# A tree stage on one core: matmul operands padded with zeros to 128 rows, and a sorted tile's last two sums moved from VectorE to GpSimd

## What is computed

```
h = h + _L1_ffn_ref(_layernorm(h), w1s, b1s, w2s, b2s)
# in _L1_ffn_ref, for each token, from the root down, 8 levels:
score  = flat_x . w1s[current] + b1s[current]
choice = (sign(score) + 1) / 2
current = current * 2 + choice + 1
# then, over the 8 nodes of its path:
out += (flat_x @ w2s[node] + b2s[node]) * gelu(|score|)
```

## Time and profile before

| | us |
|---|---|
| median of 3 runs | 4308.63 (4298.92 to 4319.09) |
| the profiled execution | 4311.47 |
| its span, first to last instruction | 4309.1 |
| TensorE busy | 3519.4 (82%) |
| VectorE busy | 2653.5 (62%) |
| ScalarE busy | 2259.2 (52%) |
| GpSimd busy | 696.7 (16%) |
| mean granted clock, share of 2.4 GHz | 0.822 |

### The profile page before, as it was taken

One profiled execution on the slowest core, in us unless ns is written; L12 is line 12 of the kernel. 1 busy time (PEld: TensorE's weight loads), 2 busy tenths in 40 slices (PEclk: granted clock), 3 DMA queues, 4 the chain that ended last, 5 costly groups with the idle time before them and its releaser, 6 DMA issues. The chain is left out here.

```text
span 4309.1 us, 60792 instructions
## 1 busy us (share of the span) xinstructions
PE 3519.4 (82%) x22648; PEld 1892.8 (44%) x22649; DVE 2653.5 (62%) x4431; ACT 2259.2 (52%) x4683; POOL 696.7 (16%) x693
## 2 busy tenths in 40 slices
PE   7549999999999999964888888759985997491896
PEld 6224444444444444332343434322224775271796
DVE  1617888887878888845877778324432333372575
ACT  1128888888888888943555555613331331120342
POOL 1310121111111111111000000024420001105443
PEclk7559999999999999986999999869997889655555
DMA  2031001111010010012000000153323122610112
GB/s 44 1 93 34 20 20 25 30 33 32 20 30 20 20 30 20 20 25 68 10 8 10 10 7 9 31 111 68 76 52 96 34 46 45 146 35 21 28 26 54
DMA packets 107095, 162.56 MB, mean 38 GB/s; under 512 B 66244, under 2 KB 89797, under 8 KB 98868
## 3 DMA queue, kind: packets, MB, share of 16 engines
q1 hardware_dynamic: 92188, 147.38, 15.5%
q0 software_dynamic: 5248, 5.71, 0.5%
q10 hardware_dynamic: 9393, 5.88, 0.4%
HBM read 85.15 MB, written 40.19 MB: 29 GB/s over the span
## 5 line engine op out<-in xcount | busy, mean ns | idle before, releaser
L970 DVE TENSOR_REDUCE att_NM<-att_ring 121x1 f32<-121x1024 f32 x1088 | 1251.4, 1214 | 315.6 <-PE att_ring L833 315.1
L905 ACT ACTIVATE att_ring<-att_ring,att_NM 121x1024 f32<-121x1024 f32 x1088 | 1193.8, 1123 | 115.4 <-DVE att_NM L970 114.8
L831 PE MATMUL att_ring<-att_q,att_k 64*121 64x512 f32 x2176 | 1166.6, 646 | 40.1 <-DVE att_Y L960 16.1
L833 PE MATMUL att_ring<-att_q,att_k 64*121 64x512 f32 x2176 | 1166.4, 646 | 0.0
L831 PEld LDWEIGHTS att_ring<-att_q,att_k 64*121 64x121 f32 x2176 | 346.2, 187 | 726.2 <-ACT att_ring L905 522.8
L1338 ACT ACTIVATE gqa_PT<-gqa_ring 121x484 f32<-121x484 f32 (+3 forms) x912 | 359.1, 450 | 197.7 <-PE gqa_ring L1265 131.9
L1382 DVE TENSOR_REDUCE gqa_NM<-gqa_ring 121x1 f32<-121x484 f32 (+1 forms) x720 | 374.8, 578 | 119.5 <-PE gqa_ring L1242 79.5
L833 PEld LDWEIGHTS att_ring<-att_q,att_k 64*121 64x121 f32 x2176 | 346.6, 187 | 0.0
L1265 PE MATMUL gqa_ring<-gqa_QS,gqa_KS 128*121 128x484 bf16 (+3 forms) x912 | 270.5, 327 | 35.9 <-ACT gqa_PT L1338 23.1
L1242 PE MATMUL gqa_ring<-gqa_KS,gqa_QS 128*121 128x484 bf16 (+1 forms) x720 | 252.6, 377 | 40.4 <-ACT gqa_PT L1338 19.1
L1722 DVE TENSOR_TENSOR moe_hh<-moe_sg,moe_p 128x484 f32<-128x484 f32 x204 | 134.2, 658 | 201.7 <-ACT moe_sg L1659 201.7
(11 more groups left out here) (439 smaller groups left out, 5505.2 us busy)
## 6 DMA issues: line engine op xcount, KB each, us to landing
moe_xw<-route_weights SPq DMA_DIRECT2D x17, 968.0 KB, 7.2
att_k<-att_k SPq DMA_DIRECT2D x32, 512.2 KB, 6.2
att_q<-att_q SPq DMA_DIRECT2D x32, 512.2 KB, 8.3
n_T<-h SPq DMA_DIRECT2D x16, 384.0 KB
by_freq<-stu_Yf SPq DMA_DIRECT2D x32, 160.0 KB
stu_YT<-by_freq SPq DMA_DIRECT2D x8, 640.0 KB, 5.6
moe_fs<-x_moe SPq DMA_DIRECT2D x4, 1028.5 KB, 11.1
sel_X<-in_x SPq DMA_DIRECT2D x4, 1024.0 KB
```

Of the source, the lines that this page charges most:

```text
L831: nc.tensor.matmul(to[0:TT, 0:512], lo[0:64, par, TT * t:TT * t + TT], mlo[0:64, par, CK * ck:CK * ck + 512], start=True, stop=True)
L833: nc.tensor.matmul(to[0:TT, 512:1024], hi[64:128, par, TT * t:TT * t + TT], mhi[64:128, par, CK * ck + 512:CK * ck + 1024], start=True, st ...
L905: nc.scalar.activation(to[0:TT, :], to[0:TT, :], ACT.Exp, bias=NM[0:TT, turn % 2, g, ck:ck + 1], accum_out=SS[0:TT, turn % 2, g, ck:ck + 1 ...
L970: nc.vector.tensor_reduce(NM[0:TT, turn % 2, g, ck:ck + 1], slot("score", turn, n)[0:TT, :], AX.X, ALU.max, negate=True).then_inc(S["max_r ...
```

## The change

The tiles `W1`, `WP`, `WG`, `xs` and `xT` get 128 rows in place of 65. Rows 65 to 127 hold zeros: GpSimd's memsets fill those of `W1`, `xs` and `xT`, and 23 more DMAs on SP copy zeros from `Z0` into `WG` and `WP`. The matmuls have the same columns, and 128 rows. `init` now counts nine memsets, and SP waits for all of them before the bias load of `W1` and so before chunk 0. The sums `pair` and `yt` move from VectorE to GpSimd, ahead of the tick, and `both` gets a second buffer; VectorE's `both` of tile n waits until `yt` of tile n - 2 is done.

```diff
-        W1 = r.sb("W1", [65, 256])
-        WP = r.sb("WP", [65, PBASE[-1] + GROUPS, 2, 64])
-        WG = r.sb("WG", [65, GROUPS, 6, 64])
+        W1 = r.sb("W1", [128, 256])
+        WP = r.sb("WP", [128, PBASE[-1] + GROUPS, 2, 64])
+        WG = r.sb("WG", [128, GROUPS, 6, 64])
...
-        xs = r.sb("xs", [65, 2, MC])
+        xs = r.sb("xs", [128, 2, MC])
...
-        xT = r.sb("xT", [65, 2, ST])
+        xT = r.sb("xT", [128, 2, ST])
...
-        both = r.sb("both", [128, 4, 64])
+        both = r.sb("both", [128, 2, 4, 64])
...
-        NINIT, NLOAD = 6, 16 * 5
-        NW2 = 6 * PAIRS + 12
+        NINIT, NLOAD = 9, 16 * 5
+        NPAIR = PBASE[-1] + GROUPS
+        NW2 = 6 * PAIRS + 12 + GROUPS // 2 + NPAIR // 6
...
                 sp.dma_start(C[:, :], consts).then_inc(S["loaded"], 16)
+                sp.dma_start(px[:, :], pidx).then_inc(S["loaded"], 16)
+                sp.wait_ge(S["init"], NINIT)
                 sp.dma_start(W1[64:65, 0:NODES], b1s.rearrange("(a n) -> a n", a=1)).then_inc(S["loaded"], 16)
-                sp.dma_start(px[:, :], pidx).then_inc(S["loaded"], 16)
...
-                    if c == NCHUNK - 1:
-                        sp.wait_ge(S["init"], NINIT)
...
+                        for k in range(GROUPS // 2):
+                            sp.dma_start(WG[65:128, 2 * k:2 * k + 2, :, :].rearrange("p g n o -> p (g n o)"), Z0[0:63, 0:768]).then_inc(S["w2_loaded"], 16)
+                        for k in range(NPAIR // 6):
+                            sp.dma_start(WP[65:128, 6 * k:6 * k + 6, :, :].rearrange("p g n o -> p (g n o)"), Z0[0:63, 0:768]).then_inc(S["w2_loaded"], 16)
...
             def _(pool):
+                nc.gpsimd.memset(W1[64:128, :], 0.0).then_inc(S["init"], 1)
+                pool.wait_ge(S["init"], 1)
+                nc.gpsimd.memset(xs[64:128, :, :], 0.0).then_inc(S["init"], 1)
+                pool.wait_ge(S["init"], 2)
                 nc.gpsimd.memset(xs[64:65, :, :], 1.0).then_inc(S["init"], 1)
...
+                nc.gpsimd.memset(xT[64:128, :, :], 0.0).then_inc(S["init"], 1)
+                pool.wait_ge(S["init"], 6)
...
+                            pool.wait_ge(S["yt_free"], 2 * i + q + 1)
+                        pool.wait_ge(S["both_added"], 2 * TG * i + j + 1 + 2)
+                        nc.gpsimd.tensor_tensor(pair[:, :, :], both[:, j % 2, 0:2, :], both[:, j % 2, 2:4, :], ALU.add).then_inc(S["pair_added"], 1)
+                        pool.wait_ge(S["pair_added"], 2 * TG * i + j + 1)
+                        nc.gpsimd.tensor_tensor(yt[:, q, j % TG, :], pair[:, 0, :], pair[:, 1, :], ALU.add).then_inc(S["y_ready"], 1)
                         pool.wait_ge(S["y_ready"], 2 * TG * i + j + 1 + TG + 1)
...
-                        nc.vector.tensor_tensor(both[:, :, :], half[:, :, :], pq[:, j % 2, :, :], ALU.add).then_inc(S["both_added"], 1)
-                        dve.wait_ge(S["both_added"], n + 1 + 2)
-                        nc.vector.tensor_tensor(pair[:, :, :], both[:, 0:2, :], both[:, 2:4, :], ALU.add).then_inc(S["pair_added"], 1)
-                        dve.wait_ge(S["pair_added"], n + 1)
-                        nc.vector.tensor_tensor(yt[:, q, j % TG, :], pair[:, 0, :], pair[:, 1, :], ALU.add).then_inc(S["y_ready"], 1)
+                        dve.wait_ge(S["y_ready"], n - 1 + TG + 1)
+                        nc.vector.tensor_tensor(both[:, j % 2, :, :], half[:, :, :], pq[:, j % 2, :, :], ALU.add).then_inc(S["both_added"], 1)
```

More of the change, by code:

```diff
@@ L2368, in _ @@
             def _(pool):
+                nc.gpsimd.memset(W1[64:128, :], 0.0).then_inc(S["init"], 1)
+                pool.wait_ge(S["init"], 1)
+                nc.gpsimd.memset(xs[64:128, :, :], 0.0).then_inc(S["init"], 1)
+                pool.wait_ge(S["init"], 2)
                 nc.gpsimd.memset(xs[64:65, :, :], 1.0).then_inc(S["init"], 1)
-                pool.wait_ge(S["init"], 1)
+                pool.wait_ge(S["init"], 3)
                 nc.gpsimd.memset(ON[:, :, 0:1], 1.0).then_inc(S["init"], 1)
-                pool.wait_ge(S["init"], 2)
+                pool.wait_ge(S["init"], 4)
                 nc.gpsimd.memset(ON[:, MK, 1:NODES], 0.0).then_inc(S["init"], 1)
-                pool.wait_ge(S["init"], 3)
-                nc.gpsimd.memset(Z0[:, :], 0.0).then_inc(S["init"], 1)
[L2376 to L2380, removed]
+                pool.wait_ge(S["init"], 5)
+                nc.gpsimd.memset(xT[64:128, :, :], 0.0).then_inc(S["init"], 1)
+                pool.wait_ge(S["init"], 6)
+                nc.gpsimd.memset(xT[64:65, :, :], 1.0).then_inc(S["init"], 1)
+                pool.wait_ge(S["init"], 7)
+                nc.gpsimd.memset(tick[:, :], 0.0).then_inc(S["init"], 1)
+                pool.wait_ge(S["init"], 8)
+                nc.gpsimd.memset(Z0[:, :], 0.0).then_inc(S["init"], 1)
+                pool.wait_ge(S["init"], 9)
                 pool.wait_ge(S["zeroed"], 16 * NZ)
```

## The result

The changed kernel takes 4336.08 us (median of 5 runs, 4332.98 to 4337.31) against 4309.62 for the kernel before, measured with it. The ratio is 1.0059, with a 95% interval from 1.0040 to 1.0077: about 26 us slower, where I had forecast 8. The profiled execution took 4336.37 us, its span is 4334.5, 25.4 longer than that of before, and the mean granted clock is 0.853.

What follows compares the result with a forecast made beforehand. The prediction took TensorE at its low clock to bound the loop. Init +2.7, padding +22, front -4 and loop -13 gave +8 us on a median of 4308.6: 4317 us, with an 8-in-10 range of 4291 to 4347.

Steps and rivals of the forecast that it cites:

- Rival 1: Loop and front: the clock stays at 0.50, TensorE keeps 2.77 us a tile; +25 us, 4334; 13%.
- rival 3: Padding transfers: 63 rows use nine of sixteen DMA engines, 40 us instead of 22; +25 us, 4334; 15%.
- What bounded the kernel: Loop of the last stage: TensorE at a clock of 0.50 sets the pace, 2.77 us a tile.
- The clock: Loop: padding to 128 rows raises TensorE's granted clock from 0.50 to 1.00, with TensorE busy 57%.
- The padding of WG and WP: Ahead of chunk 2's load: 23 transfers of zeros that nothing hides, adding 22 us.
- My low end: Padding transfers: they cost only SP's issue, 23 x 0.59 = 14 us.
- GpSimd's tile: Loop: GpSimd's two sums, tick, scatter and gaps take 2.30 us a tile.
- rival 2: Loop: GpSimd is held up beside VectorE, 0.21 us a tile, 2.99 in all; +42 us, 4351; 12%.
- The pause between halves: Loop: GpSimd's wait for its own scatters once in eight tiles is no longer hidden, 0.33 us a tile.
- The loop in all: Loop, 96 tiles: 2.63 us a tile against 2.77, 13 us gained; ends 31 us gained to 5 lost.
- Front: Scoring of chunks: VectorE no longer waits 0.30 us a chunk for TensorE, 4 us gained over 15 chunks.
- Init: Start of the stage: three more memsets send the first chunk's load out 2.7 us later, adding 2.7 us.

Runs made afterwards that it cites:

- pad_only: The changed kernel with all sums back on VectorE and one buffer for `both`, so only the padding remains: 4278.20 us, ratio 0.9928.
- pads_late: The changed kernel with the 23 padding transfers issued behind the last chunk's loads instead of ahead of chunk 2's: 4307.61 us, ratio 0.9989.
- rows125: The changed kernel with operands of 125 rows instead of 128, so 60 rows instead of 63 to a padding transfer: 4331.12 us, ratio 1.0052.
- free_late: The changed kernel, with GpSimd waiting for the scatters of an iteration's first half only after the second half's third tile: 4327.32 us, ratio 1.0033.
- sums_only: The kernel before with only the edits to `both`, `pair` and `yt`, keeping 65 rows and no padding: 4311.14 us, ratio 1.0004.
- after_tick: The changed kernel, with VectorE's `both` waiting for the tick of two tiles before instead of that tile's `yt`: 4334.44 us, ratio 1.0054.

## Why the forecast was half right

The forecast was 4317, the measured median 4336.08, a difference of 0.6% to the kernel before: slower, as I had said, and just beyond the line of 0.5% to which I gave 0.32. It lies inside a wide range (4291 to 4347), and where rivals 1 and 3 stood (4334) by chance: the clock did rise, and the transfers didn't take 40 us.

- **What bounded the kernel**: right. Freed from its clock (pad_only), the loop goes to VectorE's pace.
- **The clock**: right, and for the reason given, the filled rows. I said 1.00; in the changed kernel's loop it is 0.83 to 1.00 in stretches of 20 us, 0.92 over 260 us, and in pad_only, where VectorE sets the pace, 1.00 throughout. What makes it dip wasn't looked into. TensorE's busy share is 71% (184.29 of 260 us), not 57%: my halving of 2.77 us was wrong. At a clock of 1.00 the mean record of the products with the three pairs falls from 421 ns (before) to 275 (pad_only), to 65% and not to half; why stays open, and it cost nothing here. Rival 1 is out.
- **The padding of WG and WP**: the largest term, and mis-sized: 22 us forecast, some 27 measured (25 to 30). That nothing hides it was right (pads_late). The row I took, 205 GB/s for 64 rows, was the wrong neighbour: the DMA share of 63 rows is that of nine engines, and they run at 161 to 176 GB/s. My upper end, 29 us, from the load of 121 rows, was nearer, by luck: other rows, other engines. I had weighed the nine engines as rival 3 but priced them at 16/9 of 22 us (39, not the 40 that I wrote), as if each engine had a fixed rate. rows125 shows that it hasn't: 18.3 GB/s for each with nine busy, 14.3 with more. My low end, SP's issue alone at 14 us, could not have come out either: SP takes 21.5 us for the 23, and 21.9 in pads_late. In the changed kernel the cost is about these 21.5 us and the 6.2 by which the load behind them lands later.
- **GpSimd's tile**: 2.30 us forecast, 2.54 measured; this is the step that failed. The two sums came out close (0.48 and 0.32 against 0.43 and 0.30), the scatter right, and the gaps 0.34 together instead of 0.41, which makes up for the sums. The tick took 0.42 instead of 0.18, and that 0.24 is the difference. I had the hold-up as rival 2, with 0.21 us for it, and gave it 12%, since the 66 sums of L486 had shown none. That was a misreading of their mean. Most of them run beside nothing or beside L525 of VectorE, which reads PSUM; eight come while VectorE does its sums L514, which read both operands from SBUF, and the trace of the kernel before shows the hold-up there (duration of one in ns, least, median and most; the first line is of the whole span, the second of 1940 to 1949 us, the third of 1900 to 1960):

```profile
L486 POOL TENSOR_TENSOR n_SQ<-n_T x66: 825/825/1222, 247.3 to 3714.5; 128x384 f32<-128x384 f32 x66
L486 POOL TENSOR_TENSOR n_SQ<-n_T x8: 1020/1032/1222, 1940.0 to 1948.7; 128x384 f32<-128x384 f32 x8
L514 DVE TENSOR_TENSOR n_T<-n_T,n_R x11: 544/1175/1181, 1939.3 to 1947.8; 128x384 f32<-128x384 f32 x11
```

GpSimd's product takes 1.03 us instead of 0.83 beside such a sum, and the sum 1.18 instead of the 0.55 that L514 has where it runs alone (267.6 to 272.3 us). So rival 2 had its price in the record. I should have made it a term of the sum and asked which VectorE operation the new wait puts beside which step of GpSimd: it ties `both` to the end of `yt`, so the overlap happens in 89 of 96 tiles. Rival 2's own sum, 2.99, was too high as it doubled the unseen gap as well; the loop's mean is 2.82.
- **The pause between halves**: 0.33 us a tile forecast, (4.74 - 2.54) / 8 = 0.28 measured. That it comes out from its cover was right (free_late wins 11 of 14 us expected for half of them).
- **The loop in all**: -13 forecast, +1.5 measured, inside the ends given (-31 to +5). Two loops at TensorE's pace differ by almost as much (266.2 before, 267.3 in sums_only).
- **Front**: -4 forecast, -4.8 measured in this pair; the other traces with a front of 125 or 128 rows give -4.6 to -6.6. **Init**: the load goes out 2.6 us later from SP's first issue (4.93 against 2.32), as forecast, but of that at most 1 us is seen at chunk 2, and the averages above show none; why it isn't passed on is open.

In this pair of traces the time until chunk 2 grew by 77.6 - 47.7 = 29.9 us, for which I had 24.7. By these measured terms the sum is 29.9 - 4.8 + 1.5 = 26.6, and the forecast's 8 lacked 5 us ahead of chunk 2 and 14.5 in the loop, less 1 in the front. The direction and its reason stand: a clock's gain that is eaten by a slower engine and by transfers ahead of a stalled load.

## What to carry to other kernels

When one engine is freed, move nothing onto another until the freed kernel is measured: the padding alone was worth 55 us in the loop, and the sums moved along with it cost 56. A GpSimd step that starts just after a VectorE sum of two SBUF operands waits for it (0.17 to 0.26 us here), and a VectorE wait that starts such a sum at the end of a GpSimd step makes this happen in nearly every tile. A sum that starts inside a scatter left the scatter at 0.98 us, so ask where each wait puts the start. A fill that nobody needs for 100 us goes behind the loads that somebody waits for: two loops moved were worth 27 to 30 us.

## What was unexpected

- Rows of zeros count for the clock, and 96 of 128 do as well as 128: 1.00 over 150 us with TensorE busy 130.80; with 65 it was 0.50 at 49.76 busy of 50 (sums_only).
- The hold-up is mutual. VectorE's `half` has a mean of 0.59 us in the changed kernel and 0.43 in pad_only and 0.44 in after_tick. In 77 tiles of the changed kernel it starts inside the scatter and ends just after `pair` has started, and lasts 0.62; in the 12 where only a scatter stands beside it, 0.42. The scatter takes 0.98 in both. What holds `half` isn't shown. It costs nothing there, since VectorE waits 0.83 us a tile in any case.
- The pause of GpSimd cost nothing in the kernel before, though it is in its trace: 3.95 and then 1.60 us from scatter to scatter, two tiles in two tiles' time, against 5.05 and 2.54 after the change. A pause is hidden only while its engine can catch up behind it.
